# One head's first weight chunks moved behind a gather, and the clock-keeping products of both heads regrouped

## What is computed

```python
for _ in range(2):
    logits = _rms(x, norm_pre_w) @ compete_w.T + compete_b
    vals, idx = top_k(swapaxes(logits, 1, 2), 4)          # 16 slots choose 4 tokens each
    wgt = softmax(vals)
    wx = x @ write_w.T + write_b
    written = einsum('bsk,bskd->bsd', wgt, take(wx, idx))
    ws = _rms(ws + written, norm_post_w)
    q = x @ wq.T + bq; kk = ws @ wk.T + bk; vv = ws @ wv.T + bv
    x_b = attention(q, kk, vv) @ out_proj_w.T + out_proj_b   # 16 heads, 1024 tokens to 16 slots
    x = _rms(x + x_b, norm_post_w)
```

## Time and profile before

| | us |
|---|---|
| three runs | 1079.17, 1074.88, 1074.87 |
| their median | 1074.88 |
| the profiled execution | 1073.17 |
| its span, first to last instruction | 1071.5 |
| head 0, from its first DMA to the tail's first scores | 378.4 to 460.2 |
| head 1 | 756.2 to 834.5 |

### The profile page before, as it was taken

How to read it: one execution, slowest core, us unless ns; L and a number is a source line. 1 busy time by engine, 2 the same in 40 slices (tenths; PEclk the granted TensorE clock), 3 DMA queues, 4 the chain that set the end, 5 groups by cost and what they waited for, 6 DMA issues and landing times. The chain is left out here.

```text
span 1071.5 us, 14810 instructions
## 1 busy us (share of the span) xinstructions
PE 1007.6 (94%) x4972; PEld 571.2 (53%) x4972; DVE 724.6 (68%) x1004; ACT 574.9 (54%) x960; POOL 458.7 (43%) x214
## 2 busy tenths in 40 slices
PE   1999999999999989899999999998898999999995
PEld 0444444444444435466666666665353666666663
DVE  5999999999999732345555555554332566766664
ACT  3888888888898611235555555556112233233332
POOL 7899999999999410001111111111100133323333
PEclk9999999999999999999999999999899999999999
DMA  4456565666656689844466575645698566868664
GB/s 142 158 175 217 162 217 172 212 181 188 205 174 200 209 282 375 300 148 177 176 230 210 185 239 188 237 173 210 227 371 302 186 210 239 285 232 296 219 217 157
DMA packets 129886, 232.55 MB, mean 217 GB/s; under 512 B 8705, under 2 KB 83585, under 8 KB 129825
## 3 DMA queue, kind: packets, MB, share of 16 engines
q1 hardware_dynamic: 126880, 221.27, 61.1%
q10 hardware_dynamic: 2304, 8.39, 1.9%
q0 software_dynamic: 640, 2.10, 0.7%
HBM read 139.45 MB, written 92.28 MB: 216 GB/s over the span
## 5 line engine op out<-in xcount | busy, mean ns | idle before, releaser
L1045 PE MATMUL bank<-work 128*128 128x256 f32 (+1 forms) x992 | 237.0, 382 | 0.9 <-PEq L598 0.9
L1074 PE MATMUL bank<-work 128*128 128x512 f32 (+1 forms) x512 | 230.3, 592 | 2.1 <-ACT work L1174 1.3
L1045 PEld LDWEIGHTS bank<-work 128*128 128x128 f32 x992 | 181.3, 190 | 35.7 <-issue 16.5
L1224 POOL COPY xres<-work 128x1024 f32<-128x1024 f32 x32 | 33.4, 1043 | 326.6 <-DVE work L1156 326.6
L1234 POOL TENSOR_TENSOR work<-work 128x1024 f32<-128x1024 f32 x32 | 75.5, 2360 | 227.6 <-DVE work L1156 222.9
L453 PE MATMUL bank<-work,ident 128*128 128x512 f32 x256 | 126.9, 619 | 24.1 <-DVE work L368 22.7
L1074 PEld LDWEIGHTS bank<-work 128*128 128x128 f32 x512 | 97.1, 190 | 97.6 <-issue 91.8
L1107 DVE TENSOR_TENSOR work<-bank,sbias 128x256 f32<-128x256 f32 x64 | 27.2, 425 | 167.5 <-PE bank L1045 142.9
L438 POOL TENSOR_TENSOR work<-work 128x1024 f32<-128x1024 f32 x32 | 85.2, 2663 | 22.6 <-DVE work L360 8.2
L432 POOL TENSOR_SCALAR work<-work 128x1024 f32<-128x1024 f32 x32 | 89.1, 2785 | 4.0 <-DMA work<-in_kT 1.4
L453 PEld LDWEIGHTS bank<-work,ident 128*128 128x128 f32 x256 | 44.1, 191 | 87.2 <-issue 59.5
(11 more groups left out here) (161 smaller groups left out, 1569.3 us busy)
## 6 DMA issues: line engine op xcount, KB each, us to landing
work<-in_kT SPq DMA_DIRECT2D x32, 512.0 KB, 3.6
work<-in_xT SPq DMA_DIRECT2D x32, 512.0 KB, 3.9
x0T_scratch<-work SPq DMA_DIRECT2D x32, 512.0 KB, 3.3
x_natural_scratch<-xres SPq DMA_DIRECT2D x32, 512.0 KB, 5.1
work<-x0T_scratch SPq DMA_DIRECT2D x32, 512.0 KB, 4.6
x_natural_scratch<-work SPq DMA_DIRECT2D x32, 512.0 KB, 3.3
x1T_scratch<-work SPq DMA_DIRECT2D x32, 512.0 KB, 2.8
work<-x1T_scratch SPq DMA_DIRECT2D x32, 512.0 KB, 5.0
```

Of the source, the lines that this page charges most:

```text
L1045: last = nc.tensor.matmul(ps_s[p], xTb[p][:, c, :], Amat[:, i, :, c * 32:c * 32 + 32], start=(c == 0), stop=(c == NC - 1))
L1074: last = nc.tensor.matmul(ps_o[:, cols], attT[:, k * P:(k + 1) * P], Bmat[k][:, i, cols], start=(k == 0), stop=(k == 1), skip_group_check= ...
```

## The change

In SP's part of the head, for t = 0, the four chunks of slot 2 are sent behind the wait for the last gather and behind the loads of write_b, workspace and norm_post_w. In TensorE's part, for both heads, ten products stand ahead of the waits, two behind that for the first sum, and none behind those for the second and the third.

```diff
                 @block.sync
                 def _(sp):
-                    if t == 0:
-                        for a in range(4):
-                            first_piece(sp, 2, a)
                     sp.wait_ge(g_in[K - 1], 16)
                     for h in range(2):
...
                     if t == 0:
                         sp.dma_start(npb, npost.rearrange("(o c) -> o c", o=1).broadcast_to([P, C])).then_inc(np_in, 16)
+                    if t == 0:
+                        for a in range(4):
+                            first_piece(sp, 2, a)
                     sp.wait_ge(ob_zero, 1)
...
                         last.then_inc(lgt_ps, 1)
-                    keep_warm(psX, 8)
-                    for k in range(1, K):
-                        pe.wait_ge(xb_ok, k)
-                        keep_warm(psX, 2 if k == 1 else 1)
+                    keep_warm(psX, 10)
+                    pe.wait_ge(xb_ok, 1)
+                    keep_warm(psX, 2)
                     pe.wait_ge(xb_ok, K)
```

## The result

| | before | after |
|---|---|---|
| median of six runs, us | 1075.07 | 1082.05 |
| lowest, highest | 1074.65, 1079.17 | 1080.21, 1086.71 |
| profiled execution, its span | 1073.17, 1071.5 | 1080.21, 1078.6 |
| ratio of the times | | 1.0054, 95% interval 1.0031 to 1.0076 |

The changed kernel is slower, by 7.0 us in the medians, and the interval leaves out 1. The forecast was 2.5 us slower, and 1082.05 lies above its range (1072.5 to 1080.3).

What follows compares the result with a forecast made beforehand. From 404 to 444 the first head was taken as bound by bytes moved. Projection start -2.9 taken back, first head's end +2.5, second head 0: 1074.88 becomes 1077.4 us, range 1072.5 to 1080.3.

Steps and rivals of the forecast that it cites:

- the backlog: First head's transfer queue: four moved chunks cost 5.4 us, the room takes 2.9, so transfers run 2.5 us later.
- The term for the room: Spare transfer capacity from 396 to 404 in the first head: 2.9 us by bytes, 1.7 by busy share.
- the clock at the head's end: First head's end: no cost in the sum for a 1.2 GHz spell; only the slower rival had one, 1.8 us.
- TensorE's start: First head: transposes start at 392.1 instead of 395.02, 2.9 us sooner, and the projection at 393.5.
- the rule that the prediction took from the Trainium skill: Transposes don't count as clock work, so the clock might fall in the first projection, costing 1.8 us there.
- the direction: First head: TensorE's 2.9 us gain is taken back by a transfer-bound stretch, and the head ends 2.5 us later.
- k's first half: The moved chunks, last landing near 403.5 and wanted at 405.5 in the first head, cause no TensorE wait themselves.
- the store that VectorE waits for: First head's A_scratch store, awaited until 444.23 before, lands with the backlog; the wait ends near 446.7.
- a lag of 0.9 became 0.9 or 1.0: Comparing the two heads before: a lag at k's fourth chunk passes whole to VectorE's release.
- the slower rival: First head's queue has no room: whole 5.3 us added, plus perhaps a 1.8 us clock spell; 1080.2 to 1082, chance 0.10.
- The point of decision: First head: the slower rival holds when the eighth k chunk lands more than 5 us late.
- the aside by the Trainium skill's 358 GB/s: At that HBM rate the moved chunks would take 5.9 us and the forecast sum would be 0.5 higher.

Runs made afterwards that it cites:

- before_warm: The kernel before with two clock-keeping products ahead of the waits of each head's last product, nothing else; 1074.09 us, ratio 0.9992.
- after_quarter: The changed kernel, with only 256 of 1024 columns sent of each of k's four moved chunks; 1078.16 us, ratio 1.0022.
- chunks_on_act: The changed kernel, with k's four moved chunks issued from ScalarE's queue instead of SP's, behind the same gather wait; 1081.88 us, ratio 1.0063.
- products_only: The kernel before with only the new order of the clock-keeping products; k's chunks stay at the head's start; 1073.96 us, ratio 0.9985.
- after_warm: The changed kernel plus, in the first head, two clock-keeping products ahead of q's last product's wait and three before the tail's first x tile; 1079.35 us, ratio 1.0029.
- chunks_at_g0: The changed kernel, with k's four chunks sent once the first gather has landed instead of behind the last; 1079.03 us, ratio 1.0036.
- chunks_only: The kernel before with only k's four chunks moved behind the gathers; products in their old order; 1082.06 us, ratio 1.0051.
- small_first: Against products_only: first head's write_b, workspace, norm_post_w and out-bias loads sent directly behind k's chunks, not the last gather; 1082.88 us, ratio 1.0049.
- after_tiny: The changed kernel, with only 8 of 1024 columns sent of each of k's four moved chunks; 1078.04 us, ratio 1.0006.

## Why the prediction was wrong

The step that failed is the backlog, **2.5 us**, and what was left out behind it. The term for the room was too large, and the clock at the head's end stood in the sum with nothing. Together the head came to +5.6 where +2.5 was forecast.

*TensorE's start: right in this profile.* Forecast 2.9 us sooner; measured 2.8 at the transposes and 2.7 at the projection. The idle time before the transposes was to be 1.1 and is 1.36. But part of the gain is the spell that the profile of before happened to have: in before_warm, with the same code up to there, the clock did not fall behind 2.48 us of idle time and the projection started at 14.6, 1.2 us behind the changed kernel's 13.4. And with the new order the clock did fall in the projection in after_quarter, behind 1.20 us, and in chunks_on_act, behind 1.12. By the rule that the prediction took from the Trainium skill ("TensorE: Matmul & The Clock Gate", transpose mode), the four transposes do not break the pause; that fits these two profiles and not the changed kernel's own, where a like pause left the clock at 1.00.

*Right: the direction.* TensorE's gain went into waits for k's and v's chunks, and the first projection's lead did not reach the end. The products of q were to start 0.5 us later than before; they started 2.1 later. TensorE did not wait for k's first half, as forecast, but only just: its fourth chunk landed at 406.0 and not near 403.5, some half a microsecond ahead of its use.

*Wrong: the room.* The step "the bytes leave 8 x (1 - 249 / 387) = 2.9 us ... I am nearer to the bytes" took the rate of another stretch for this one. With the queue full the stretch from 396 to 404 moved 332 GB/s (335 in products_only). The busy share of 0.79 gave 1.7 us, a backlog of 3.6, and the measured lag is 5.0 at k's eighth chunk, 3.9 at the first chunk of wq and 4.0 at the last addition: 5.3 less 4.0 leaves a room of 1.3, and of 0.5 if before_warm (65.4) is taken for the kernel before. The stretch is also what an earlier start would use: products_only fills it to a share of 0.98 with no extra byte. Part of that may be why the room was not there; how much, the scatter of 1.4 us between like profiles hides.

*Luck: the store that VectorE waits for.* It landed 2.5 us later (447.53 - 381.06 against 444.23 - 380.30), the forecast to the tenth. The other profiles with the four chunks behind the gathers or beside them say that this is no confirmation: VectorE was released 4.1 us later than before in after_warm and 4.0 to 4.3 later in chunks_at_g0 and chunks_on_act, and then made its three additions in one row; in chunks_only, with a spell on q's last product like the changed kernel, it was 2.8. In all of them the last addition is at 70.2 to 70.5. The step from one pair of heads, that "a lag of 0.9 became 0.9 or 1.0", did not carry over: the lag of 5.0 at k's eighth chunk was 3.9 at the first chunk of wq.

*Wrong: the chain stopped one store too soon.* In the changed kernel's profile the eighth store of A and the store to B_scratch behind it ended last, 4.0 late. The copy of q's sixth product waited 2.90 us for a staging buffer, that is for the first store; q's last product stood behind that copy and ran at 1.2 GHz, and its own copy and the eighth store followed. In before the sixth did not wait; the seventh waited 0.39 us and the eighth 1.45:

```profile
438.42 0.69 DVE L756 COPY work<-bank 128x512 f32<-128x512 f32 x1 [1.45 <-DMA A_scratch<-work]
```

With that product at full speed again (after_warm) the last addition did not move, so this chain was not the only thing that held it: the transfers were as late by themselves.

*Wrong: the clock priced at nothing in the forecast.* The spell was in the slower rival, "at worst on the path". The idle time ahead of the head's last product grew from 1.74 to 3.28 us because the groups before it were not slowed by a spell of their own (7.07 and 8.65 in two pieces before, 14.02 in one now) while the load behind the additions was 3.9 later. In before the spell stood on the groups, in the shadow of a wait; in the changed kernel one stood on the product with nothing behind it: 1.7 us, and after_warm gives them back.

*The point of decision was right, if barely:* the slower rival was to hold when the eighth k chunk lands more than 5 us late. It landed 5.0 late, its second sign (k's second half after 411) was there at 412.0, TensorE had waits of 2.59 and 3.28 us with a spell behind each, and 1082.05 is at the top of that rival's 1080.2 to 1082. I gave it 0.10.

*A sum to put right:* the aside by the Trainium skill's 358 GB/s ("DMA: Bandwidth & Descriptors", Specifications) used that figure for the price alone. Used for the room too, 8 x (1 - 249 / 358) = 2.4 us, it is an estimate of 0.9 over the forecast, not 0.5. The changed kernel moved 386 GB/s from 404 to 436, so this trace disagrees with the figure as well.

*Open:* 4.0 + 1.7 is 5.7; the medians differ by 7.0 and the spans by 7.1. The second head, whose code differs between the runs at most in clock-keeping products, was 78.2 to 83.2 us long over these profiles, and the first head began within 1.3 us. That spread is large enough for the rest; nothing here shows that it is the rest. One source of it can be seen: in every profile the second head begins at a granted clock of 0.50, carried over from the tail, for 3.2 us in before (24 records in 12.12 us, where the changed kernel's first head took 10.57) and 4.6 in the changed kernel, whose projection there starts at 14.1 instead of 13.4.

## What to carry to other kernels

In this stretch the busy share told the room better than the rate against the rate of another stretch did, and both told too much. Room may be wanted twice: an edit that starts the consumers sooner fills it as well as one that adds bytes. Moving a load out of the way of a short gather pays only if it lands in time that nobody else can use; here it went into the queue that ends the stage. When one landmark comes out as forecast, look at it in the other runs before it counts as a confirmation. When a lag is followed to the stage's end, follow it to the last of a row of waits, and ask which idle time stands ahead of the last instruction of the fast engine.

## What the runs showed of the hardware

- The granted clock fell or did not behind nearly the same idle time, in one kernel: 3.16 us without a fall, 3.12 with one (products_only). On the head's last product the price was between 1.6 (5.25 for 3.69, chunks_only) and 3.0 us (6.64, products_only). In before_warm TensorE still idled 1.21 and 1.39 us behind the two filling products, so there they cost nothing.
- Four gathers of 128 rows that were met by up to 3.2 MB of other loads took about twice as long from issue to landing, 7.6 to 8.4 us (small_first) instead of 3.6 to 3.9 (after), and VectorE waited 7.24 us for the first one.
- Four issues in SP's queue took 1.86 us for transfers of 8 columns each (after_tiny) and 2.03 for whole chunks (after). In chunks_on_act 2.3 us of sooner issue brought the landing of the stream's first chunk 0.1 us forward (26.3 for 26.4).
